# A gather and interaction kernel: on ScalarE, the copy of the turned unit put ahead of the word split of the next one

## What is computed

```python
def interaction(bottom_output, embeddings):            # (2048, 128), (2048, 26, 128)
    all_emb = jnp.concatenate([bottom_output[:, None, :], embeddings], axis=1)   # 27 rows of 128
    gram = jnp.einsum('bfd,bgd->bfg', all_emb, all_emb)
    return gram[:, _TRIU_I, _TRIU_J]                   # 351 pairs

e = jnp.stack([tbl_0[ids[:, 0]], ..., tbl_25[ids[:, 25]]], axis=1)
z = interaction(r_bottom_output, e)
h = jnp.concatenate([z, r_bottom_output], axis=1)      # 479
h = jnp.maximum(h @ W_top1 + b_top1, 0.0)              # 512
h = jnp.maximum(h @ W_top2 + b_top2, 0.0)              # 256
y = h @ W_top3                                         # (2048, 1)
```

## Time and profile before

| | |
|---|---|
| median of 3 runs | 355.23 us (355.19 to 356.12) |
| the profiled execution | 354.72 us, of it span 353.0 us |
| PE busy | 330.9 us, 94% of the span |
| ACT busy | 225.7 us, 64% |
| POOL busy | 253.6 us, 72% |
| DVE busy | 249.8 us, 71% |
| instructions | 13726 |

### The profile page before, as it was taken

How to read it: one execution, slowest core, us unless ns; L and a number is a source line. 1 busy time by engine, 2 the same in 40 slices (tenths; PEclk the granted TensorE clock), 3 DMA queues, 4 the chain that set the end, 5 groups by cost and what they waited for, 6 DMA issues and landing times.

```text
span 353.0 us, 13726 instructions
## 1 busy us (share of the span) xinstructions
PE 330.9 (94%) x5840; PEld 299.8 (85%) x5840; DVE 249.8 (71%) x740; ACT 225.7 (64%) x373; POOL 253.6 (72%) x270
## 2 busy tenths in 40 slices
PE   2988999899999999999999999999999999969996
PEld 1867899899999988999998988999989989848775
DVE  3999999696875975679665976679765977330412
ACT  4796785428777577757676677757866758755222
POOL 5777777777777777777777777777777777777700
PEclk9999999999999999999999999999999999989999
DMA  7767667257567877496884886547775546553200
GB/s 212 226 195 232 193 171 214 60 116 127 111 98 154 148 119 131 91 148 118 144 115 106 150 116 163 106 109 115 137 159 118 116 84 128 115 114 84 54 11 1
DMA packets 74555, 45.08 MB, mean 128 GB/s; under 512 B 58432, under 2 KB 66624, under 8 KB 74496
## 3 DMA queue, kind: packets, MB, share of 16 engines
q1 hardware_dynamic: 65504, 26.84, 39.6%
q0 software_dynamic: 8320, 17.06, 20.5%
q10 hardware_dynamic: 672, 0.33, 0.4%
HBM read 31.08 MB, written 0.01 MB: 88 GB/s over the span
## 4 chain that ended last, share of the span: by engine, by line
POOL 63%; issue 21%; PE 8%; DMA 5%; DVE 2%; ACT 1%; ACTq 0%; DVEq 0%
POOL X L453 62%; DMA X<-in_table_dram,rows_sb 4%; PE h_ps L552 2%; POOL Z L442 1%; PE gram_ps L496 1%; PE h_ps L549 1%; PE h_ps L597 1%; DMA rows_sb<-in_rows_dram 1%; PE xt_ps L471 1%; ACT planes L877 1%; DVE Z L738 1%; ACT XT L705 0%; PE zt_ps L534 0%; PE hot_ps L583 0%; PE h_ps L583 0%
## 5 line engine op out<-in xcount | busy, mean ns | idle before, releaser
L453 POOL DMA_INDIRECT X<-in_table_dram,rows_sb x256 | 247.7, 967 | 79.8 <-issue 76.2
L730 DVE TENSOR_SCALAR onehot<-ids_wide,row_value 128x288 fp32r<-128x288 int16 (+2 forms) x593 | 189.2, 388 | 52.8 <-PE hot_ps L518 37.3
L518 PE MATMUL hot_ps<-onehot,tab 128*128 128x288 f32 (+2 forms) x932 | 144.5, 307 | 12.1 <-DVE tab L797 7.3
L518 PEld LDWEIGHTS hot_ps<-onehot,tab 128*128 128x128 f32 x932 | 131.3, 193 | 15.9 <-issue 10.2
L705 ACT COPY XT<-turned 128x512 int16<-128x512 int16 x100 | 79.4, 874 | 16.2 <-DMA turned<-planes 15.9
L877 ACT COPY planes<-X 128x1024 int16<-128x1024 int16 x50 | 53.3, 1066 | 41.8 <-DMA X<-in_table_dram,rows_sb 41.7
L496 PEld LDWEIGHTS gram_ps<-XT 128*27 128x27 f32 x4096 | 45.0, 105 | 20.4 <-issue 12.8
L496 PE MATMUL gram_ps<-XT 128*27 128x26 f32 x4096 | 55.1, 192 | 5.2 <-ACT XT L705 3.2
L888 ACT COPY XT<-hot_ps 128x288 f32<-128x288 f32 (+3 forms) x66 | 39.1, 654 | 23.4 <-PE hot_ps L518 23.4
L518 PE MATMUL xt_ps<-onehot,tab 128*128 128x288 f32 (+1 forms) x288 | 45.6, 306 | 0.0
L552 PE MATMUL h_ps<-stage_sb,w_sb 128*128 128x256 f32 (+3 forms) x192 | 44.5, 367 | 0.0
(11 more groups left out here) (58 smaller groups left out, 125.7 us busy)
## 6 DMA issues: line engine op xcount, KB each, us to landing
stage_sb<-in_hot_dram SPq DMA_DIRECT2D x19, 256.0 KB, 4.8
X<-in_table_dram,rows_sb POOLq DMA_INDIRECT x256
ids_wide<-in_hot_ids_dram SPq DMA_DIRECT2D x8, 360.0 KB
ids_wide<-in_hot_ids_dram SPq DMA_DIRECT2D x4, 400.0 KB
bottomT<-in_bottom_t_dram SPq DMA_DIRECT2D x8, 128.0 KB, 3.9
w_sb<-in_w_dram SPq DMA_DIRECT2D x4, 256.0 KB, 3.9
stage_sb<-in_hot_dram SPq DMA_DIRECT2D x7, 128.0 KB, 2.9
turned<-planes SPq DMA_TRANSPOSE x50
```

What stands on the lines that cost most here:

```text
L453: pool.indirect_dma_start(X[:, n % RING, k, :], None, table, bass.IndirectOffsetOnAxis(idx[:, column:column + 1], 0)).then_inc(gathered[n ...
L518: mm = pe.matmul(hot_bank(i)[:, 0:width(n)], tab[u][:, part, D * c:D * (c + 1)], onehot[p % ONEHOTS][:, c - BITES[u][h], 0:width(n)], star ...
L730: compared = dve.tensor_scalar(onehot[p % ONEHOTS][:, c - BITES[u][h], 0:width(n)], ids_wide[:, k, 0:width(n)], row_value[:, c:c + 1], Non ...
```

## The change

In `step(b)` of ScalarE, `move(b + 2)` goes from the end of the step to the place just ahead of `split_words(b + 3)`. No instruction is added or removed. The lists of the other engines stay as they are, and so do the buffers.

```diff
@@ -942,6 +942,8 @@
                     if is_last(p) and ASKED[p][0] in placed_in(b):
                         place_hot(ASKED[p][0])
                     one_hot_share(p + ONEHOTS)
+                if b + LEAD - 1 in BY_DMA:
+                    move(b + LEAD - 1)
                 split_words(b + LEAD)
                 if j == 2:
                     place_bottom(t + 1)
@@ -949,8 +951,6 @@
                     split_first(q)
                 if b + LEAD < TURN_FROM:
                     move(b + LEAD)
-                if b + LEAD - 1 in BY_DMA:
-                    move(b + LEAD - 1)
 
             def last_blocks():
```

## The result

The changed kernel takes 446.5 us in the median of six runs (441.52 to 451.72), the kernel before 355.21 us in six runs beside it (354.11 to 358.14). The ratio is 1.252, with a 95% interval of 1.243 to 1.260. (Both kernels have slower executions now and then, here those of 449.97 and 451.72 us, and all ratios are taken without them.) The forecast was 431 us in a range of 404 to 458. The profiled execution of the changed kernel took 445.98 us, its span 444.2 us.

What follows compares the result with a forecast made beforehand. TensorE and the stream of gathers were taken to set the old pace of 4.96 us a unit; 48 rounds of 1.41 + 1.04 + 4.10 = 6.55 us add 76.3 us to 354.72, giving 431 us, range 404 to 458.

Steps and rivals of the forecast that it cites:

- The loop: ScalarE's copy, split and transpose flight follow one another without overlap between units: 6.55 us a round against 4.96; chance 0.84.
- The pieces: On ScalarE, 1.41 us from copy start to split start and 1.04 us for the split, within each round.
- The 48 rounds: From the copy of unit 10 to that of unit 58, each 6.55 us instead of 4.96: +76.3 us.
- The flight: From the end of ScalarE's split to the start of the copy waiting for its DMA transpose, taken as 4.1 us.
- waiting copies are a selection of slow flights: Argument that copies marked as waiting show long transpose times, so the mean of all lies below their 4.04 to 5.29 us.
- The eight marked waits: Copies after the first shown waiting for their transpose in the old kernel, with flights between 4.04 and 5.29 us.
- The short gaps: Split to copy without a wait in the old kernel, units 34 and 30: 3.26 and 3.42 us, ceilings for the flight.
- Rival A: A transpose alone has a short flight, 3.26 us or a little less, giving 380 to 400 us; chance 0.06.
- Rival B: Flight under 2.51 us, so the round fits the present pace: about 350 us; chance 0.02 faster, 0.01 within 0.3%.
- Rival C: TensorE's clock falls when idle and TensorE becomes the bound: 479 us; 0.06 for over 458, shared with long flights.
- TensorE's waits: TensorE should wait for the copy in most blocks, some 70 us in all, its busy share falling to about 78%.

## Why the prediction was right, point by point

**The loop** held as told, and it alone set the time: 50 waits, the chain of copy, split and flight, and the runs that open it without undoing the edit.

**The pieces** held where they came from rows: 1.41 to 1.44 us from copy to split, 1.03 to 1.05 for the split. The 48 rounds were counted rightly.

**The flight** was the mis-sized term: 4.1 us taken, 4.48 found in those 48 rounds (6.945 - 2.46). 48 x 0.395 us longer a round is +19.0 us, the start -3.4 and the end -0.7, which leads from the forecast's 431.0 to 445.9 for the profiled execution's 445.98. The step that failed is the sentence that waiting copies are a selection of slow flights. The eight marked waits had a mean of 4.49 us, and so had the 48 flights. They stand where ScalarE comes to the copy early, which is the state that the changed kernel is always in. This reading is argued, the two means are measured; that they agree to 0.01 us is luck, since the eight lie from 4.04 to 5.29. The short gaps of 3.26 and 3.42 us were rare rather than typical: in both the next gather started some 0.5 us after the split and not 0.27, and no packet stood on q8. In the changed kernel the flights of units 10 to 19, while GpSimd did not yet wait for splits, had a mean of 3.97 us, and those of units 24 to 57, when a split released each set of gathers, 4.64. Four of the first ten (units 10, 12, 14 and 18), with the next gather 0.8 to 1.1 us after the split, took 3.26 to 3.51 us; of the later ones none was under 3.91. So the place of the gather beside the split fits the difference, but no run of the whole kernel moved it out of the way, so for this kernel the cause is read from one trace and not tested.

**Rival A**, a flight that is short when a transpose is alone, was wrong as I put it. Transposes were alone throughout the changed kernel and no shorter. With the gather out of the way as well it is 3.1 us. A's 3.26 us was about the floor, which the changed kernel itself reached in three flights of 50 (3.26 to 3.32 us), and not the mean.

**Rival B** and the Trainium skill's figure ("DMA: Bandwidth & Descriptors", section "Latency and other measured facts") did not come true. The estimate of 1.6 us by it is half of the shortest flight in any run with whole units, 3.08 us. Even a quarter of the bytes took 2.35 us at the least. In the undisturbed flight of 3.09 us shown above the first packet of the transpose starts 1.20 us after the split and the last ends at 2.62, so that the moving of the data, 1.4 us, is under half of the flight.

**Rival C** came in part, and without price. The clock fell after idle stretches, as here in the changed kernel (TensorE in order of time, and busy times of 4 us with the granted clock behind POOL's):

```profile
241.18 0.96 PE L496 MATMUL gram_ps<-XT 128*27 128x26 f32 x64 [3.40 <-ACT XT L705]
...
243.09 2.77 PE L552 MATMUL h_ps<-stage_sb,w_sb 128*128 128x256 f32 x6
...
246.50 1.56 PE L552 MATMUL h_ps<-stage_sb,w_sb 128*128 128x256 f32 x6
```

```profile
240.00:244.00 4.00, 2.82 (x69) 2.41 (x70) 0.00 (x0) 2.63 (x4) 1.43 (x2) 0.50 0.27 57
...
248.00:252.00 4.00, 4.00 (x89) 3.79 (x88) 3.99 (x13) 2.30 (x4) 1.85 (x1) 1.00 0.57 38
```

Behind a wait of 3.40 us six products of layer 1 take 2.77 us at a granted clock of 0.50 (1.2 of 2.4 GHz) and 1.56 us once it is back. Over the run TensorE's busy time grew from 330.9 to 354.9 us, and by the runs with extra work all of that lay in the slack of the rounds.

**TensorE's waits** were told wrongly in one point. I had some 70 us of waiting for the copy in most blocks. It was 17.4 us in nine waits, and 36.6 us in ten for placements (17.6, 17.3 and 1.7 at the tile `xt_ps`). Its busy share fell to 80%, where I had about 78%. The placements are queued on ScalarE behind the waiting copy, and with the banks and group bounds they hold TensorE as much as the copy does. TensorE then waits seldom and long, and behind such a wait its clock fell, as shown. The time did not depend on it.

## What to carry to other kernels

In a list that runs in order, a wait put ahead of the instruction that starts the next round of the same work closes a loop. Its price is the full sum of the pieces less the present pace, in every round, however slack both instructions were before. Ask how many units lie between the start of a transfer and the wait for it, since one more unit of distance (356 us) or every other step (357 us) was enough to lose nothing. For the length of a transfer that will be waited for every time, the mean of the waits that are marked now was the better guide here than the shortest gaps. Look also at what the same semaphore sets off beside the transfer, and at the packets of the other queues.

## What the runs showed of the hardware

- A DMA transpose of 256 KB from SBUF to SBUF, from the end of the instruction that releases it to the start of the one that waits for it, took 3.09 to 3.17 us in all 18 flights with neither a gather nor an instruction packet beside it. In the one followed through, 1.20 us pass before its first packet and 0.47 after its last.
- A gather issued 0.27 us after its release made this 3.89 to 4.11 us in 15 flights with nothing else in their way. Its first 1024 packets came as before, and its last 32 only among the gather's. How much the gathers moved mattered less: one of four or all four gave 4.59 and 4.46 us in the mean.
- A 16 KB packet on the instruction queue that falls into the flight went with flights of up to 4.84 us without gathers and of up to 5.96 us with one.
- Half of the bytes took 0.63 us off and a quarter 1.00 us, between flights with the same gather beside them (medians of 4.09, 3.46 and 3.09 us). SyncE's own issue stayed at 1.23 us in the median of all of these runs with whole units.
